# Graph layer and expert layer on one core: the order of TensorE's work inside an edge group

## What is computed

```
x1  = layernorm(x)
xw  = x1 @ W                                   # per convolution
deg = segment_sum(w, dst); dinv = rsqrt(deg)   # self loops included
out = segment_sum(xw[src] * (dinv[src]*w*dinv[dst])[:, None], dst) + b
graph: relu(conv(W1)) -> conv(W2) -> batch norm over rows -> + x1 -> relu
x = x + graph(x);   x = x + experts(layernorm(x))
```

## Time and profile before

| | |
|---|---|
| median of 3 runs | 2931.6 us (2924.9 to 2938.58) |
| the profiled execution | 2933.57 us, its span 2931.8 us |
| PE busy | 2116.7 us (72%), granted clock 0.848 on average |
| POOL busy | 1661.1 us (57%) |
| DVE busy | 890.2 us (30%) |
| stages of 40 groups | the first 574 to 1368 us, the second 1380 to 2255 us |

### The profile page before, as it was taken

How to read it: one execution, slowest core, us unless ns; L and a number is a source line. 1 busy time by engine, 2 the same in 40 slices (tenths; PEclk the granted TensorE clock), 3 DMA queues, 4 the chain that set the end, 5 groups by cost and what they waited for, 6 DMA issues and landing times.

```text
span 2931.8 us, 33886 instructions
## 1 busy us (share of the span) xinstructions
PE 2116.7 (72%) x10594; PEld 1512.5 (52%) x10595; DVE 890.2 (30%) x2641; ACT 378.5 (13%) x1053; POOL 1661.1 (57%) x1732
## 2 busy tenths in 40 slices
PE   0541028987888867766787887888887558999887
PEld 0430013455555556655455555555555444888886
DVE  8940000022221222323122322322323864333322
ACT  7010000000000000000000000000001561344333
POOL 1877760066666666664666665665653511666665
PEclk9975568998999987777898998988988556999999
DMA  9990024454555534333454544544545332777775
GB/s 332 329 296 1 0 57 136 133 158 144 161 158 154 159 101 119 102 116 117 140 153 149 149 141 135 151 143 141 151 144 167 115 114 82 172 193 189 181 178 123
DMA packets 264403, 431.36 MB, mean 147 GB/s; under 512 B 39664, under 2 KB 147887, under 8 KB 264143
## 3 DMA queue, kind: packets, MB, share of 16 engines
q1 hardware_dynamic: 181455, 253.80, 27.4%
q0 software_dynamic: 81088, 173.80, 23.1%
q10 hardware_dynamic: 1728, 2.13, 0.2%
HBM read 339.36 MB, written 91.16 MB: 147 GB/s over the span
## 4 chain that ended last, share of the span: by engine, by line
PE 42%; issue 18%; another core or an unknown queue 17%; DVE 12%; DMA 5%; POOL 3%; POOLq 1%; DVEq 1%; ACT 0%; SPq 0%; ACTq 0%
PE psum L1404 17%; PE psum L1419 14%; DMA ACC<-rows_for_experts,ACC 4%; PE psum L1359 3%; DVE arena L1015 3%; PE psum L1523 2%; PE psum L1531 2%; POOL out_dram L591 2%; PE psum L1498 2%; DMA out_dram<-ACC 1%; DVE stats L1111 1%; PE psum L1514 1%; DVE edge_cols L1105 1%; DVE X L1108 1%
## 5 line engine op out<-in xcount | busy, mean ns | idle before, releaser
L535 POOL DMA_INDIRECT arena<-conv_rows,edge_cols x1120 | 1064.2, 950 | 780.2 <-issue 318.4
L1404 PE MATMUL psum<-arena,X 128*128 128x512 f32 x1568 | 812.1, 647 | 134.7 <-issue 77.2
L1419 PEld LDWEIGHTS psum<-arena 128*128 128x128 f32 x4480 | 628.4, 207 | 415.8 <-issue 405.4
L1419 PE MATMUL psum<-arena 128*128 128x128 f32 x4480 | 668.2, 293 | 221.0 <-issue 207.6
L1404 PEld LDWEIGHTS psum<-arena,X 128*128 128x128 f32 x1568 | 298.1, 207 | 402.8 <-issue 339.0
L522 POOL DMA_INDIRECT pair_weights<-scale_b,mean_b x224 | 247.3, 1104 | 135.9 <-issue 68.0
L1039 DVE TENSOR_TENSOR ACC<-ACC,psum 128x256 f32 x80 | 33.8, 422 | 908.6 <-remote 456.7
L1015 DVE TENSOR_SCALAR arena<-iota,edge_cols 128x128 f32<-128x128 f32 x1120 | 294.1, 367 | 5.8 <-issue 5.7
L1523 PE MATMUL psum<-ACC,arena 128*128 128x128 f32 x1680 | 210.9, 280 | 0.2 <-DVE ACC L1248 0.2
L591 POOL DMA_INDIRECT out_dram<-ACC x105 | 167.9, 1599 | 74.6 <-issue 47.0
L1523 PEld LDWEIGHTS psum<-ACC,arena 128*128 128x128 f32 x1680 | 201.6, 196 | 0.6 <-issue 0.6
(11 more groups left out here) (280 smaller groups left out, 1388.2 us busy)
## 6 DMA issues: line engine op xcount, KB each, us to landing
arena<-pair_weights SPq DMA_DIRECT2D x392, 256.0 KB
arena<-in_L_ffn_W_dram SPq DMA_DIRECT2D x113, 512.0 KB, 7.9
pair_weights<-zeros SPq DMA_DIRECT2D x4, 12544.0 KB, 42.4
arena<-conv_rows,edge_cols POOLq DMA_INDIRECT x1120
conv_rows<-X SPq DMA_DIRECT2D x14, 896.0 KB
X<-in_x_dram SPq DMA_DIRECT2D x12, 896.0 KB, 10.7
rows_for_experts<-ACC SPq DMA_DIRECT2D x7, 910.0 KB, 4.2
out_dram<-X SPq DMA_DIRECT2D x6, 896.0 KB
```

The costliest lines, as they stand in the source:

```text
L535: pool.indirect_dma_start(G[:, n * D:(n + 1) * D], None, y_tab[layer], bass.IndirectOffsetOnAxis(srcT[:, t:t + 1], 0)).then_inc(gathered[n ...
L1404: ins = m.matmul(bank(6 + c, BW), X[:, t * D + c * P:t * D + (c + 1) * P], A_in[:, u * BW:(u + 1) * BW], start=(t == 0), stop=(t == NT - 1))
L1419: ins = m.matmul(bank(2 * (k % 2) + c, P), G[:, n * D + c * P:n * D + (c + 1) * P], S[:, n * P:(n + 1) * P], start=(j == 0), stop=(j == GT ...
```

## The change

Two places change, on PE and on DVE. On PE a group was: after some of its tiles a dense unit, after others a linear step, the 14 tiles spread over the whole group. Now the 14 tiles come first, `summed` is raised, and then come the dense units with the linear steps between them. On DVE `add_group(k)` stood behind the group's blocks and its `finish` steps; now it stands right behind `build(k + 1)`. POOL's, SP's and ACT's lists are the same.

```
--- DVE, aggregate
                             if k + 1 < GG:
                                 build(k + 1)
+                            add_group(k)
                             while blocks < NB and (blocks + 1) * NT <= first_unit + units:
                                 add_block(blocks)
...
                             for i in FINISH[layer][1][k]:
                                 finish(layer, i)
-                            add_group(k)
--- PE, aggregate
                                 for c in range(KC):
                                     ins = m.matmul(...)            # the tile, line 1419
-                                if j == GT - 1:
-                                    ins.then_inc(summed, 1)
-                                for d in range(units * j // GT, units * (j + 1) // GT):
+                            ins.then_inc(summed, 1)
+                            tiles = FINISH[layer][1][k]
+                            for d in range(max(units, len(tiles))):
+                                if d < units:
                                     dense(first_unit + d)
-                                if layer == 1 and k and j == 2 and 0 in FINISH[1][1][k - 1]:
+                                if layer == 1 and k and d == 0 and 0 in FINISH[1][1][k - 1]:
                                     mean_of_first()
-                                if j % 4 == 2 and j // 4 < len(FINISH[layer][1][k]):
-                                    i = FINISH[layer][1][k][j // 4]
+                                if d < len(tiles):
...
-                                    linear(layer, i)
+                                    linear(layer, tiles[d])
```

More of the change, by code:

```diff
@@ L1420, in aggregate @@
                                                    S[:, n * P:(n + 1) * P], start=(j == 0), stop=(j == GT - 1))
-                                if j == GT - 1:
-                                    ins.then_inc(summed, 1)
-                                for d in range(units * j // GT, units * (j + 1) // GT):
+                            ins.then_inc(summed, 1)
+                            tiles = FINISH[layer][1][k]
+                            for d in range(max(units, len(tiles))):
+                                if d < units:
                                     dense(first_unit + d)
-                                if layer == 1 and k and j == 2 and 0 in FINISH[1][1][k - 1]:
+                                if layer == 1 and k and d == 0 and 0 in FINISH[1][1][k - 1]:
                                     mean_of_first()
-                                if j % 4 == 2 and j // 4 < len(FINISH[layer][1][k]):
-                                    i = FINISH[layer][1][k][j // 4]
-                                    blocks = NB if layer == 0 else blocks_under(FINISH[1][0][i])
+                                if d < len(tiles):
+                                    blocks = NB if layer == 0 else blocks_under(FINISH[1][0][tiles[d]])
                                     if DG * layer + blocks:
                                         pe.wait_ge(dense_added, DG * layer + BG * blocks)
-                                    linear(layer, i)
+                                    linear(layer, tiles[d])
                         pe.wait_ge(added, GG * (layer + 1))
```

## The result

The changed kernel is slower: 2985.87 us median (2983.91 to 2992.7) against 2928.25 us (2923.66 to 2938.58) for the kernel before in the same comparison, a ratio of 1.0195, 95% interval 1.0167 to 1.0224. That is +58 us where +124 us were forecast. The direction, the engine and the line are the forecast ones; the size is less than half of it.

The account below looks back on a forecast made before the run. The bound was taken to be PE's raises, held while POOL's gathers run and let go behind the last gather, so POOL pauses. 57 + 71 + 0 - 4 = +124 us on 2933.57 gave 3058 us, range 2925 to 3120.

Parts of the forecast that it names:

- The hold's beginning: In each group, PE's raises are held from 7 to 8.4 us after POOL's first gather until behind the last gather.
- The run-ahead of 36: PE runs 36 more records once the hold begins, then about one record per us until the release.
- high bound: One record per 1.4 us, run-ahead 34, half clock also for the first units: +221 us in all.
- The records left: Groups with units, first convolution: 13.5 of 76 records left at the release, at half clock, 3.0 us.
- the first term: Groups with units, first convolution: period 23.1 against 20.38 us, +2.7 us on 21 groups, +57 us.
- Second convolution: All 37 groups of the second convolution: period 23.5 against 21.58 us on average, +1.9 us each, +71 us.
- Linear steps: Groups with three linear steps, first convolution: sum ready before the release and let go with it, period 20.1, 0 us.
- edges: Group 0's sum comes earlier, so the third gather starts 7 us earlier; the next group gives back 3: -4 us.
- DVE and SP: DVE's earlier addition and SP's closer raises: both 0, between -5 and +20 us in all depending on a block's addition.
- No change: Rival, 2935 us (2917 to 2946): full clock for what is left and a run-ahead of 41; chance 0.09.
- The tiles fit: Rival, 2875 us: all 56 tile records done by the release, every period 20.1, run-ahead above 49 records; chance 0.08.
- Prompt sums: Rival, 2690 us: a sum raised early gets through at once, POOL never stops between groups, period 17.5; chance 0.04.

Follow-up runs that it names:

- g7: Changed kernel with 7 gathers per group instead of 14, each pair of tiles multiplying the same gathered rows; 2441.54 us, kernel before 2975.34 us on that chip.
- e3: Kernel before with PE doing eleven tiles, then units and linear steps, then three tiles; 0.9872 of the kernel before with the hold, 0.9978 without.
- f4: Changed kernel with one matmul per edge tile, 28 tile records per group instead of 56; with the hold 2886.49 us, 0.986 of the kernel before, single run.
- i1: Kernel before with PE doing one tile, then units and linear steps, then 13 tiles; with the hold 3002.48 us, 1.0031 of the kernel before.
- i5: Kernel before with PE doing five tiles, then units and linear steps, then nine tiles; with the hold 2917.72 us, 0.9747 of the kernel before.
- the changed kernel's second run: The changed kernel, unaltered, beside the kernel before on another chip, which holds the raises; 3022.66 us against 2972.85 us, 1.0163.
- f1: PE's list of the changed kernel with DVE's list of the kernel before, with the hold; 2991.92 us, 1.0213 of the kernel before.
- e1: PE's list of the changed kernel with DVE's list of the kernel before, without the hold; 2516.75 us, 1.0024 of the kernel before.

## Why the direction was right and the size wrong

**What bounds it: right here, and not everywhere.** POOL's pause between groups, ended by PE's held raise, is the bound in the runs near 2930 to 2990 us; g7 shows that the gathers hold the raises. In the runs near 2500 us there is no hold. Nothing in the one trace told that such a state exists.

**The hold's beginning (7 to 8.4 us after the first gather, nothing out behind it): the step that failed.** The changed kernel's raises are on time at 10.1 us, e3's are 3 us late at 7.5. The hold is no switch. As the late raises of e3 and f4 can be read, PE's records are let out in order, some 35 in the first 9 to 12 us, then 1 to 2 per us, then less than 1 until the release. A raise is late when PE has been faster than that. Units (2.3 records per us) are not; the old order's mix of units and tiles (5.2 per us) is from some 7 us on, and that is what the earlier trace rows showed.

**The run-ahead of 36: right, but counted from the wrong point.** PE can be some 36 records ahead of what is out. The forecast let nothing out behind 8.3 us and had 55 records through at 12.3 us, then one per us: 62.5. Measured, 20 are out at 10.1 us; with some 12 more by the release, an estimate with the rates of e3, 32 + 36 = 68, which is what the trace has. By the same sum i1 would have 24 + 12 + 36 = 72, four left (its trace has 5.8 on average), and i5 40 + 5 + 36 = 81, more than the group's 76. A smaller error went the other way: the first units behind a release ran at half clock (0.50 from 948.3 to 951.7), so 20 unit records took 10.57 us where i5's took 8.75. The forecast had that in its high bound alone.

**The records left: 13.5 forecast, 8 measured (7.4 on average), at the forecast clock.** This is the mis-sized term of the sum. Half clock was right (0.51, eight records in 1.6 us). So the first term is +1.25 us on 21 groups, +26 and not +57.

**Second convolution, +71 forecast, +25 measured.** The same step (16 records left forecast, 10.8 measured), and a second one: the term gave all groups the same loss. In this trace the changed kernel starts the convolution without it. Its eighth first gather from 1450.48 on, in the timeline of POOL, is

```profile
1592.97 0.96 POOL L535 DMA_INDIRECT arena<-conv_rows,edge_cols  x1 [3.77 <-PE psum L1419]
```

so (1592.97 - 1450.48) / 7 = 20.4 us for seven groups, and has (2273.86 - 1592.97) / 30 = 22.7 in those behind them. PE comes into this convolution ahead: behind the release near 1450 only 4 of the 20 unit records are still before it, the others having run in the crawl ahead of it. The lead shrinks from group to group, to 13 and 16 unit records in its fourth and fifth first gathers from 1450.48 on,

```profile
1510.06 6.12 PE L1404 MATMUL psum<-arena,X 128*128 128x512 f32 x13 [0.61 <-issue]
...
1531.19 7.03 PE L1404 MATMUL psum<-arena,X 128*128 128x512 f32 x16
```

and all 20 from the eighth on, which is where tile records begin to be left and the loss sets in. So PE passes some records fewer in a period than a group has, and a lead hides that until it is spent. How long it lasts differs: in the changed kernel's second run all 20 are before PE from the third of these groups on, and the seven take 21.9 us each; in f1 from the sixth on, and they take 20.8.

**Linear steps 0, edges -4, DVE and SP 0:** measured +3, -5, and by f1 nothing to be seen from DVE. The 0 does not hold throughout: POOL's idle time is 2.8 us at both ends of the stretch with three steps, but up to 4.2 us in its groups 31 to 35, where up to 5 tile records are left behind the release, and the changed kernel's second run has a period of 21.25 there. The prediction named a growing stretch as the sign against this term. Whether the turns to DVE are the reason stays open.

**The rivals.** "No change" (2935) came closer to the result than the forecast (3058), with 8 records left at full clock; the 8 were right, the clock was not. "The tiles fit" needed all 76 records passed by the release, and 68 were. By the prediction's own count, from 8.3 us to the release, PE passed 51 records on average, more than the 49 that were to decide for this rival; but it had 16.6 behind it at 8.3 us and not 19, and needed all 76. "Prompt sums" is true on other occasions, at 2500 to 2517 us and not 2690, as the stage ahead of the convolutions is faster there too (POOL's third group of gathers begins near 428 us, not 587).

**What would show it.** POOL's idle time in the stretch with units is 3.2 to 5.0 us and not 5 to 6, ended by L1419 with a record close by, as said. The single records on L1419 take 4.5 us and not 6 to 8.

## What to carry to other kernels

Where an engine's raise is late, compare when its records end with when the waiting engines see them, count the records between, and do so at two different speeds of the engine before calling it a time: one order of work can't tell a rate from a moment. Where an engine's pause ends with a release, count the instructions that are left at that moment and order the work so that few are: here five tiles, then the long units, then nine tiles. Eleven tiles ahead made the units' raises late, one did next to nothing. And before a change of a per cent is judged, see whether the kernel has another regime in which its bound is a different one, and compare ratios only where the baseline is the same: here it moved by 2% between chips within one regime.

## What the runs showed of the hardware that was not expected

- The same kernel takes 2499 to 2512 us at some times and 2927 to 2992 us at others, on four chips by the numbers that the runs carry; numbers 1 and 14 each showed both, 15 only the lower time and 9 only the higher. At the higher time PE's raises are held while POOL issues indirect transfers, and the page has no landing times for the gathers and the dense loads; at the lower one it has them (3.1 and 3.4 us) and nothing is held. What decides between the two stays open, and so does whether the missing landing times are a part of it. The trace of before has 290 of the 1281 updates of one of the gathers' semaphores that e1's has. All runs were recorded by the profiler, so it is not excluded that the recording itself makes the hold; whether there is one without it is not shown.
- With the hold, POOL that doesn't pause gains nothing: two groups back to back take 17.6 and 22.9 us.
- The changed kernel itself was not run without the hold; PE's part of it alone gives 1.0024 there. The DVE part alone was not run with the hold.
